# Self-attention's query, key and value projections: three float32r products of high and low parts in place of one float32 product

## What is computed

```python
x = layernorm(x)                               # 8 x 64 x 512
q = einsum('bsd,hde->bhse', x, Wq1)            # 16 heads of 32: one 512 x 512 matrix
k = einsum('btd,hde->bhte', x, Wk1)
v = einsum('btd,hde->bhte', x, Wv1) + bv1
scores = q k^T * 32**-0.5, causal mask, p = softmax(scores)
sa = p v
x = layernorm(sa + x)                          # then cross-attention on ctx_1024, and the rest
```

## Time and profile before

| | us |
|---|---|
| median of three runs | 1539.83 |
| lowest and highest | 1535.94, 1539.97 |
| the profiled execution | 1537.29 |
| its span | 1536.1 |
| TensorE busy | 1472.6 (96%) |
| VectorE busy | 868.0 (57%) |
| ScalarE busy | 666.4 (43%) |
| GpSimd busy | 253.3 (16%) |

### The profile page before, as it was taken

How to read it: one execution, slowest core, us unless ns; L and a number is a source line. 1 busy time by engine, 2 the same in 40 slices (tenths; PEclk the granted TensorE clock), 3 DMA queues, 4 the chain that set the end, 5 groups by cost and what they waited for, 6 DMA issues and landing times.

```text
span 1536.1 us, 30237 instructions
## 1 busy us (share of the span) xinstructions
PE 1472.6 (96%) x12864; PEld 1136.1 (74%) x12864; DVE 868.0 (57%) x1340; ACT 666.4 (43%) x1239; POOL 253.3 (16%) x290
## 2 busy tenths in 40 slices
PE   9789899999999999999999988998989999999998
PEld 5469788887888887888887776786478766666665
DVE  3642332543544544535346466545966788888886
ACT  1423333343343443433434444452424366666663
POOL 1233222212121211121212230602061000000000
PEclk9899999999999999999999999999989899999999
DMA  7012211010101010101011035305100079999992
GB/s 260 1 46 76 66 46 42 22 46 22 46 22 42 25 42 22 46 22 46 22 43 46 27 123 186 115 0 209 38 3 30 1 252 345 342 343 335 343 345 75
DMA packets 85220, 159.99 MB, mean 104 GB/s; under 512 B 4576, under 2 KB 25056, under 8 KB 85088
## 3 DMA queue, kind: packets, MB, share of 16 engines
q1 hardware_dynamic: 85088, 158.06, 29.8%
HBM read 157.00 MB, written 1.05 MB: 103 GB/s over the span
## 4 chain that ended last, share of the span: by engine, by line
PE 86%; DVE 8%; ACT 2%; POOL 2%; issue 2%; ACTq 0%; DVEq 0%; POOLq 0%
PE ring L608 17%; PE ring L598 17%; PE ring L1942 9%; PE turnbank L644 6%; PE pv L1966 4%; PE sc L625 4%; PE pv L663 3%; PE pv L1942 3%; PE sc L1573 3%; PE sc L1141 3%; PE pv L1974 2%; PE ring L1153 2%; PE pv L672 1%; PE sc L358 1%; PE sc L431 1%
## 5 line engine op out<-in xcount | busy, mean ns | idle before, releaser
L562 POOL TENSOR_TENSOR x_l<-raw,x_h 128x384 fp32r<-128x384 f32 (+1 forms) x160 | 162.6, 1048 | 709.9 <-ACT x_h L555 709.8
L1779 DVE TENSOR_TENSOR w_lo<-w_raw,w_hi 128x2048 fp32r<-128x2048 f32 x88 | 200.4, 2284 | 24.6 <-ACT w_hi L2032 24.6
L754 ACT ACTIVATE prob<-sc,nm 128x384 f32<-128x384 f32 (+1 forms) x256 | 153.6, 610 | 99.2 <-DVE nm L848 57.5
L608 PE MATMUL ring<-wv_h,x_h 128*128 128x512 f32 (+2 forms) x520 | 191.1, 367 | 0.0
L598 PE MATMUL ring<-x_h,wk_h 128*128 128x384 f32 (+1 forms) x512 | 185.9, 363 | 4.9 <-POOL x_l L562 4.9
L843 DVE TENSOR_REDUCE nm<-sc 128x2 f32<-128x898 f32 (+1 forms) x128 | 128.1, 1021 | 103.5 <-PE sc L625 103.5
L608 PE MATMUL ring<-wv_h,x_l 128*128 128x512 f32 (+2 forms) x520 | 181.0, 348 | 0.0
L608 PE MATMUL ring<-wv_l,x_h 128*128 128x512 f32 (+2 forms) x520 | 180.5, 347 | 0.0
L598 PE MATMUL ring<-x_h,wk_l 128*128 128x384 f32 (+1 forms) x512 | 176.6, 345 | 0.0
L598 PE MATMUL ring<-x_l,wk_h 128*128 128x384 f32 (+1 forms) x512 | 176.0, 344 | 0.0
L2032 ACT CAST w_hi<-w_raw 128x2048 fp32r<-128x2048 f32 x88 | 167.6, 1907 | 18.4 <-PE pv L1966 15.5
(11 more groups left out here) (484 smaller groups left out, 2633.2 us busy)
## 6 DMA issues: line engine op xcount, KB each, us to landing
w_raw<-in_ew SPq DMA_DIRECT2D x96, 1024.0 KB, 5.4
raw<-in_ctxT SPq DMA_DIRECT2D x30, 768.0 KB, 4.3
raw<-in_ctxT SPq DMA_DIRECT2D x10, 900.0 KB, 4.7
wf1b<-in_wf SPq DMA_DIRECT2D x1, 2560.0 KB, 10.4
wf2b<-in_wf SPq DMA_DIRECT2D x1, 2560.0 KB, 16.6
wf1a<-in_wf SPq DMA_DIRECT2D x1, 1536.0 KB, 9.4
wf2a<-in_wf SPq DMA_DIRECT2D x1, 1536.0 KB, 12.9
xin<-in_x SPq DMA_DIRECT2D x1, 1024.0 KB, 5.7
```

The costliest lines, as they stand in the source:

```text
L562: pool.tensor_tensor(x_l[x % 3][:, c, 0:w], raw[x % 3][:, c, 0:w], x_h[x % 2][:, c, 0:w].bitcast(F32), ALU.subtract)\
L608: m = pe.matmul(ring[k % 2][0:rows, 0:cols.stop - cols.start], xt[:, c, t1:t1 + rows], wt[:, c, cols], start=c == 0 and n == 0, stop=c == ...
L754: act.activation(prob[:, i, 0:WIDTHS[r]], sc[:, i, score_columns(r)], ACT.Exp, bias=nm[:, b % 2, r, h:h + 1], accum_out=psum[:, b % 2, r, ...
L1779: return eng.tensor_tensor(w_lo[n % NSLOT][:, :, :], w_raw[n % NSLOT][:, :, :], w_hi[i % 4][:, :, :].bitcast(F32), ALU.subtract)
```

## The change

The three matrices and the transposed rows are each split into a high part (rounded to float32r by a cast on ScalarE) and a low part (what is left, by a subtraction on VectorE, into float32r). Each product becomes three: high x high, high x low, low x high. Every sum over c and the three products stays in one PSUM bank.

- The query matrix goes to banks 4 to 7 in three passes: all 16 high x high products, c outermost and the four banks in turn, as each `n1_h` chunk is ready; then 16 products with `n1_l`, in the same order; then 16 with the low part of the matrix, bank by bank. The key matrix goes to banks 0 to 3, bank by bank, twelve products each, and the value products get three terms too.
- ScalarE now starts with two casts of matrices and makes all four casts of rows; VectorE makes the low parts. The low part of a matrix overwrites the matrix.
- Buffers for the new parts lie over ones that are used later (`s1` and `pT1`, `p1`, `sa`, `x_h[1]`); two waits guard that, in `shifted(0)` and `act_split(1)`.
- Four semaphores are folded into others, to make room for the new ones; order and work there are the same.

```diff
+    w1_lo = [at(f"w1_lo{i}", R + 90112 + 8192 * i, [P, NC, D], F32R) for i in range(3)]
+    w1_hi = [at(f"w1_hi{i}", R + place, [P, NC, D], F32R) for i, place in enumerate((188992, 132128, 123936))]
+    n1_h = at("n1_h", R + 115744, [P, NC, TOK], F32R)
+    n1_l = at("n1_l", R + 81920, [P, NC, TOK], F32R)
...
 dve_self
-        for c in (0, 1):
-            dve.wait_ge(sem("turned"), 1)
-            dve.tensor_copy(nT[:, c, :], bank[c]).then_inc(sem("turned_copied"), 1)
+        def weights_low(i):
+            dve.wait_ge(sem("w1_high"), i + 1)
+            dve.tensor_tensor(w1_lo[i][:, :, :], w_in[i][:, :, :], w1_hi[i][:, :, :].bitcast(F32), ALU.subtract)\
+               .then_inc(sem("w1_low"), 1)
+
+        for c in range(NC):
+            dve.wait_ge(sem("n1_high"), c + 1)
+            dve.tensor_tensor(n1_l[:, c, :], bank[c], n1_h[:, c, :].bitcast(F32), ALU.subtract).then_inc(sem("turned_copied"), 1)
+        weights_low(0)
+        weights_low(1)
         dve.wait_ge(sem("rows_loaded"), 64)
...
-            dve.tensor_scalar(qT1[:, c, :], bank[c], SCALE, None, ALU.mult).then_inc(sem("self_qk_copied"), 1)
+            dve.tensor_scalar(qT1[:, c, :], bank[4 + c], SCALE, None, ALU.mult).then_inc(sem("self_qk_copied"), 1)
+        weights_low(2)
         dve.wait_ge(sem("split_high"), 1)
...
-            dve.tensor_copy(kT1[:, c, :], bank[4 + c]).then_inc(sem("self_qk_copied"), 1)
+            dve.tensor_copy(kT1[:, c, :], bank[c]).then_inc(sem("self_qk_copied"), 1)
...
             dve.wait_ge(sem("scores_done"), t + 1)
+            if t == 0:
+                dve.wait_ge(sem("self_proj_done"), NC)
...
 act_self
-        for c in (2, 3):
+        def weights_high(i):
+            act.wait_ge(sem(f"matrix{i}_loaded"), 16)
+            act.copy(w1_hi[i][:, :, :], w_in[i][:, :, :]).then_inc(sem("w1_high"), 1)
+
+        weights_high(0)
+        weights_high(1)
+        for c in range(NC):
             act.wait_ge(sem("turned"), 1)
-            act.copy(nT[:, c, :], bank[c]).then_inc(sem("turned_copied"), 1)
+            act.copy(n1_h[:, c, :], bank[c]).then_inc(sem("n1_high"), 1)
+        weights_high(2)
...
 pe_self
-        pe.wait_ge(sem("turned_copied"), 4)
-        for i, b0 in enumerate((0, 4)):
-            pe.wait_ge(sem(f"matrix{i}_loaded"), 16)
+        def block_of(w, j, c):
+            return w[:, c, j * P:(j + 1) * P]
+
+        pe.wait_ge(sem("w1_high"), 1)
+        for c in range(NC):
+            pe.wait_ge(sem("n1_high"), c + 1)
             for j in range(NC):
-                for c in range(NC):
-                    m = pe.matmul(bank[b0 + j], w_in[i][:, c, j * P:(j + 1) * P], nT[:, c, :], start=c == 0, stop=c == NC - 1)
-                m.then_inc(sem("self_proj_done"), 1)
+                pe.matmul(bank[4 + j], block_of(w1_hi[0], j, c), n1_h[:, c, :], start=c == 0, stop=False)
+        for c in range(NC):
+            pe.wait_ge(sem("turned_copied"), c + 1)
+            for j in range(NC):
+                pe.matmul(bank[4 + j], block_of(w1_hi[0], j, c), n1_l[:, c, :], start=False, stop=False)
+        pe.wait_ge(sem("w1_low"), 1)
+        for j in range(NC):
+            for c in range(NC):
+                m = pe.matmul(bank[4 + j], block_of(w1_lo[0], j, c), n1_h[:, c, :], start=False, stop=c == NC - 1)
+            m.then_inc(sem("self_proj_done"), 1)
+        pe.wait_ge(sem("w1_low"), 2)
+        for j in range(NC):
+            for c in range(NC):
+                for n, (w, x) in enumerate(((w1_hi[1], n1_h), (w1_hi[1], n1_l), (w1_lo[1], n1_h))):
+                    m = pe.matmul(bank[j], block_of(w, j, c), x[:, c, :], start=c == 0 and n == 0, stop=c == NC - 1 and n == 2)
+            m.then_inc(sem("self_proj_done"), 1)
...
-                m = pe.matmul(bank[4 + t], nT[:, c, t * P:(t + 1) * P], w_in[2][:, c, :], start=c == 0, stop=c == NC - 1)
+                for n, (x, w) in enumerate(((n1_h, w1_hi[2]), (n1_h, w1_lo[2]), (n1_l, w1_hi[2]))):
+                    m = pe.matmul(bank[4 + t], x[:, c, t * P:(t + 1) * P], w[:, c, :], start=c == 0 and n == 0,
+                                  stop=c == NC - 1 and n == 2)
...
         scores(0)
-        pe.wait_ge(sem("matrix2_loaded"), 16)
+        pe.wait_ge(sem("w1_low"), 3)
...
 act_split
+        if x == 1:
+            act.wait_ge(sem("self_proj_done"), 2 * NC + NT)
```

More of the change, by code:

```diff
@@ L295, in act_self @@
     def act_self(act):
-        for c in (2, 3):
+        def weights_high(i):
[4 more added lines that the diff above has]
+        for c in range(NC):
             act.wait_ge(sem("turned"), 1)
-            act.copy(nT[:, c, :], bank[c]).then_inc(sem("turned_copied"), 1)
+            act.copy(n1_h[:, c, :], bank[c]).then_inc(sem("n1_high"), 1)
+        weights_high(2)
         for c in (2, 3):
             act.wait_ge(sem("self_proj_done"), c + 1)
-            act.mul(qT1[:, c, :], bank[c], SCALE).then_inc(sem("self_qk_copied"), 1)
+            act.mul(qT1[:, c, :], bank[4 + c], SCALE).then_inc(sem("self_qk_copied"), 1)
         act.wait_ge(sem("kv2_loaded"), 32)
@@ L305, in act_self @@
             act.wait_ge(sem("self_proj_done"), NC + c + 1)
-            act.copy(kT1[:, c, :], bank[4 + c]).then_inc(sem("self_qk_copied"), 1)
+            act.copy(kT1[:, c, :], bank[c]).then_inc(sem("self_qk_copied"), 1)
         def exponentials(t):
@@ L1245, in pool_masks @@
         pool.iota(zint[:, 1, :], pattern=[[1, P]], base=0, channel_multiplier=0).then_inc(sem("indices_ready"), 1)
-        pool.wait_ge(sem("xor_ready"), 1)
+        pool.wait_ge(sem("indices_ready"), 2)
         link(pool.affine_select(out=Z[:, 0, :], in_=Z[:, 0, :], compare_op=ALU.is_gt, fill=0.0, base=0,
@@ L1278, in dve_xor @@
         link(dve.tensor_copy(Z[:, 0, :], zint[:, 0, :]))
-        dve.tensor_copy(Z[:, 1, :], zint[:, 0, :]).then_inc(sem("xor_ready"), 1)
+        dve.tensor_copy(Z[:, 1, :], zint[:, 0, :]).then_inc(sem("indices_ready"), 1)
     MASK1, IDENT = len(LEVELS), len(LEVELS) + 1
@@ L1360, in dve_delta @@
         dve.wait_ge(sem("mix_tanh"), 1)
-        dve.scalar_tensor_tensor(mixr[:, :], trow[:, :], 1.0, mixr[:, :], ALU.add, ALU.mult).then_inc(sem("mix_silu"), 1)
+        dve.scalar_tensor_tensor(mixr[:, :], trow[:, :], 1.0, mixr[:, :], ALU.add, ALU.mult).then_inc(sem("mix_conv"), 1)
         dve.wait_ge(sem("mix_tanh"), 2)
@@ L1492, in act_delta @@
         act.activation(trow[:, :], mixr[:, :], ACT.Tanh, scale=0.5).then_inc(sem("mix_tanh"), 1)
-        act.wait_ge(sem("mix_silu"), 1)
+        act.wait_ge(sem("mix_conv"), 2)
         act.wait_ge(sem("hbias_ready"), 1)
@@ L1831, in dve_experts @@
                                   over_width(pos[:, t, e], CAP), ALU.is_equal).then_inc(sem("slots_ready"), 1)
-        dve.wait_ge(sem("margin_exp"), 1)
+        dve.wait_ge(sem("margin_ready"), 2)
         link(dve.tensor_scalar(rw[:, 0, :], rw[:, 1, :], 1.0, None, ALU.add))
@@ L2042, in act_experts @@
         act.wait_ge(sem("margin_ready"), 1)
-        act.activation(rw[:, 1, :], rw[:, 1, :], ACT.Exp).then_inc(sem("margin_exp"), 1)
+        act.activation(rw[:, 1, :], rw[:, 1, :], ACT.Exp).then_inc(sem("margin_ready"), 1)
         act_high(act, 2)
```

## The result

| | before | after |
|---|---|---|
| median, ten runs each | 1539.98 us | 1532.01 us |
| lowest, highest | 1535.94, 1543.90 | 1527.54, 1537.15 |
| the profiled execution | 1537.29 | 1537.15 |
| its first 128x512 product of the projections | 13.88 | 14.51 |
| scores(0) | 42.29 | 37.74 |

The ratio is 0.9947, 95% interval 0.9932 to 0.9962: the change takes 5.9 to 10.5 us off, 8.0 by the medians, where 5.2 were forecast. The two profiled executions are 0.1 us apart all the same. That has to be read before anything else: the profiled execution of the kernel after was the slowest of its ten, at a mean granted clock of 0.975, where the profiled execution of the kernel before had 0.982. The full kernels' runs all count as fast; of the fronts further down, where one low stretch of the clock lifts a run over 1.5% above the fastest, all runs are used.

What follows compares the result with a forecast made beforehand. TensorE was taken to hold 86% of the chain, its query and key products bounding the start. 5.6 saved, 0.5 lost, 0.75 gained, 0.66 lost give 5.2 us: 1539.83 - 5.2 = 1534.6 us, range 1531.0 to 1538.8.

Steps and rivals of the forecast that it cites:

- The bound, and the products: Query and key projections on TensorE: 96 float32r products at 0.229 us replace 32 float32 ones, 27.74 to 22.1, saving 5.6 us.
- rival of three quarters exactly: Query and key products: float32r at half a float32 record, 0.217 us each, gain 6.5 us, total 1533.3; chance 0.04.
- Banks in turn: First two query passes change bank at each product: forecast no cost; rival of a whole record, 1539.7 us, chance 0.08.
- The bound of 5.1 us: Upper bound on the cost of changing banks at each product, if nothing overlapped: 32 x 0.16 us.
- The start: First query product: row casts queue behind the key matrix's landing and cast, so TensorE starts at 14.4 us, 0.5 later.
- Cover: Splits and copies beside the projections hide behind TensorE's passes; key copies end by 33.7, last key product 36.5: 2.8 us cover.
- The values: Value products: VectorE's 11.8 us sets the pace; shorter products only remove ScalarE's wait, gain 0.75 us.
- The low clock behind the idle time: Transposes of the probabilities: after 4.3 us of TensorE idle time they start at low clock, costing 0.66 us.
- Part 4: the rest: From 62.72 us on VectorE leads, unchanged; later loads and casts move with the work; folded semaphores cost nothing.
- The sum: Whole gain: 5.6 - 0.5 + 0.75 - 0.66 = 5.2 us.
- So the gain is carried to the end: Everything behind the self-attention moves with it, so the whole kernel gains the same 5.2 us.
- a sign of being wrong: Refuting sign: the time after the fourth norm moves by something else than the time before it.

Runs made afterwards that it cites:

- fronts: Kernels cut off behind the cross-attention's query projection, the rest of the layer left out; medians 114.42 us for the kernel before, 110.22 us for the changed one.
- rows first: Changed kernel with ScalarE casting the four row chunks before the key matrix: median 1528.45 us, ratio 0.9930 to the kernel before.
- float32 values in the new front: Changed kernel cut behind the query projection, value products in float32 as before, without the rows' low part or the value matrix's split: 110.19 us.
- front before: Kernel before, cut behind the cross-attention's query projection: median 114.42 us; the four profiles of this front include full kernels with the same front.
- changed front: Changed kernel, cut behind the cross-attention's query projection, the rest of the layer left out: median 110.22 us.
- before again: Kernel before timed once more, no edit: ratio 0.9993 to the kernel before.
- before, folded: Kernel before with only the change's folded semaphores: ratio 1.0004 to the kernel before.
- after again: Changed kernel timed once more, no edit: median 1531.34 us, ratio 0.9953 to the kernel before.
- kept at work: Changed kernel with 14 products of the identity on TensorE while it waits ahead of the transposes: median 1529.47 us, ratio 0.9932 to the kernel before.
- both edits: Changed kernel with rows cast before the key matrix and 14 identity products ahead of the transposes: 1527.87 us, ratio 0.9922; cut behind the query projection, 106.39 us.
- by bank: Changed kernel with the query matrix bank by bank, twelve products each: 1536.15 us, ratio 0.9982 to the kernel before; cut behind the query projection, 115.57 us.

## Why the prediction was right or wrong

**The bound, and the products.** Right. 27.74 us became 22.6 (14.51 to 36.67 + 0.40): 5.2 us saved, against 5.6. The rows' 0.229 us a product was 0.232 here; over 96 products that is most of the difference. The rival of three quarters exactly needed 0.217 us a product and would have saved 6.9; the measured 0.232 decides against it. The Trainium skill (FP8 and Floating Point Precision, TensorE Precision Notes) says that true FP32 takes four passes; that three float32r products then cost three quarters of it does not hold in this trace, where they cost four fifths.

**Banks in turn.** Right: they cost nothing. The bound of 5.1 us was an empty one.

**The start.** The mechanism was right. ScalarE's wait for the key matrix and its cast (11.98 to 13.88) held the rows' casts; 14.51 was measured, 14.4 forecast. Casting the rows first gave 1.3 us back, at every milestone to the transposes.

**Cover.** Right. VectorE's key copies ended 5 us before the last key product (`wv2` landed at about 26.8 us, not 28.1).

**The values.** Right. VectorE's 11.8 us from scores(0) to the second exponential came out as forecast, and the float32 values in the new front moved the transposes by 0.85 us.

**The low clock behind the idle time.** Right, and nearly in size. The idle time ahead of the transposes was 3.71 us (4.3 forecast), and the clock fell there in every profile that had it. From the transposes to the third mask add it takes 2.25 us in the mean of the four profiles of the front before (1.94 to 2.57), and 2.98 in the three of the front after (2.76 to 3.20): 0.7 us lost, where 0.66 was forecast. The working said that the scores behind the transposes don't count; they do a little, 1.24 us instead of 0.86 at the full clock.

It would be easy to find a larger price in the two first profiles: the low stretch of the kernel after lasts 30.7 us and ends over the context products, and from the third mask add to the query projection's last record the execution took 44.85 us against 43.71 before. But that is the difference of two executions. To the end of the query projection the four profiles of the front before take 44.3 to 46.1 us, mean 45.4, and the three of the front after 44.7 to 45.4, mean 45.1. So inside the stage what follows did move with the work, as "Part 4: the rest" said.

**The sum.** Forecast for the stage 5.2 us. Between the means of the same four and three profiles the gain is 4.6 us at scores(0) (5.1 forecast), 5.5 at the transposes (5.85), 4.8 at the third mask add and 5.1 at the end of the query projection. The first two profiles alone would have said 3.7 there. The fronts' medians gave 4.2, and in them are the changed front's runs at a lower clock than its profiled one. So the stage gave what was forecast, or a little less.

**The step that doesn't hold.** It is the last one of Part 4, "So the gain is carried to the end": the whole layer gained 8.0 us and not the stage's 5. The prediction named this itself as a sign of being wrong, that the time behind the fourth norm moves by something else than the time before it. Why it does is not shown.

**What isn't explained.** The full runs gained more than the fronts, and this is called the surplus here: 8.0 and 7.3 us in two comparisons, 7.9 with a standard error of 0.7 over 79 runs of the kernel before and 21 of the one after. Some 3 to 4 us are made somewhere the fronts don't show (3.9 by the means, with a standard error of 0.9). The profiles don't show them either. From the start of the query projection's last record to the end of the span:

| kernel | us | of it at the low clock | less half of that |
|---|---|---|---|
| before | 1429.6 | 37.5 | 1410.9 |
| before again | 1426.3 | 27.3 | 1412.7 |
| before, folded | 1432.7 | 44.4 | 1410.5 |
| after | 1433.2 | 41.0 | 1412.7 |
| after again | 1428.5 | 34.1 | 1411.5 |
| rows first | 1426.0 | 27.3 | 1412.4 |
| kept at work | 1431.7 | 41.0 | 1411.2 |
| both edits | 1432.1 | 41.0 | 1411.6 |
| by bank | 1431.9 | 41.0 | 1411.4 |

(The low time is counted to some 8 us before the end, where all are alike.) The last column is the same for all within 2.2 us and favours neither side: behind the front the same work takes nearly the same time, and most of the 7.2 us by which the tails differ follows the low clock. That accounts for most of the spread of the runs, and for about half of the 3.5 us that the kernel after had lost again in its first profile (3.65 us ahead at the front's end, 0.1 at the end of the run): its tail was 3.6 us longer than that of the kernel before, of which 3.5 us more at the low clock make 1.8.

My theory was that luck of the clock makes the surplus too. The granted clock on record for each run speaks against it in its simple form. The 69 runs of the kernel before that have one show 59.2 us of low time in the mean (standard error 0.9), the 21 of the kernel after 58.3 (1.8): the changed kernel doesn't meet less of it. A line through the 133 such runs of the six full kernels gives 0.31 us of time for each us at the low clock, and at equal low time the gain is 7.7 us (standard error 0.4). It also accounts for the two first profiled executions, equal in time: the one after had 21 us more of low time, which is worth 6.4 us. Nor does the whole layer bank by bank fit the theory: its front is 1.2 us slower than before and the whole is 2.8 us faster by the ratio, the same surplus of 3 to 4 us. The folded semaphores are excluded.

One hint is left. The changed front by itself has more low time than the front before, 25.9 us against 20.2 in the mean of its runs, and the whole kernels have the same. The part behind the front would then have 6.6 us less (standard error 3.2). The same sum for the kernels bank by bank and with both edits gives 7.4 (4.2) and 5.9 us (5.7) less, and their surplus is 3.8 us each. At 0.31 to 0.5 us for each us this would be 2 to 3 us, the greater part of the surplus. But it is an estimate with errors nearly as large as itself, all three lean on the same five runs of the front before, and the tails of the profiles in the table don't show it. The profiled executions of the changed kernels may not be typical either: in three cases of six they were the slowest of their runs (of ten, of six and of six). Whether the low stretches behind the front really become fewer, and why a changed front should do that, remains open.

**The forecast as a whole.** 1532.01 lies in the range, and the sign was right. The mechanism was right for the 5 us of the stage. The gain was 8.0, not 5.2, and no step of the working had the other 3; that the median stayed within the range all the same is owed to the range's width. With the stage's gain alone it would have been about 1535.

## What to carry to other kernels

Splitting a float32 product into three float32r ones saves a fifth of its time, not a quarter, and only where the products set the pace: here the query and key matrices gave nearly all of it, and the value products only 0.85 us of a wait, which the low clock behind the longer idle time took back. Order the passes by when their operands are ready, the low parts last, or waiting for them costs more than the split saves. And when a stage gets shorter on TensorE but not on the engine that it then waits for, price the longer idle time: it cost 0.7 us here, and products of the identity put in it gave 1.0 back in the fronts, nearly as much as the better order of the casts (1.2). Last, don't read a cause from a piece that is on the chain in one profile and not in another: profile the unchanged kernel twice first.

## What the runs showed of the hardware

- The granted clock fell at a different point of the same program in each execution. Over nine full profiles the tail behind the front held 27 to 44 us at the low clock, and runs of one full kernel spread over 7 to 10 us; a comparison of two profiles alone can't measure a change of 5 us: the first two were 0.1 us apart. The fronts spread over 1.2 to 3.0 us. The Trainium skill (TensorE: Matmul & The Clock Gate, What's actually happening) says that the chip's look at activity runs free and isn't restarted by a kernel; the moving low stretches agree.
- Ahead of the first products, four profiles with an idle time of 1.88 to 1.98 us kept the full clock. The one with 2.37 us had a fall at 14.7 us, 0.3 us after the first product, and the 6.7 us of the kernels bank by bank had one in both (17.4 and 17.7 us).
- Ahead of the transposes of the probabilities, all six profiles with an idle time of 3.7 us had a fall between 1.1 us before the transposes and 0.4 us after their start. Of five with 1.97 or 1.98 us three had one, 0.7 to 1.5 us after the start. The three with products of the identity, where 0.59 us was left, had none for 9 us.
- Over the runs of the full kernels a microsecond at the low clock went with 0.31 us more of time; it would be 0.5 if TensorE set the pace throughout.
- Products that go to another one of four banks each time start 0.23 us apart, like those in one bank.
